# Fourier layers of a vision tower on one core: the inverse row product of a pair in one piece on PE

## The chip, the cores and the metric

One NeuronCore of a Trainium2 chip (trn2). The metric is the device time of one launch in microseconds. The core has engines that run side by side and meet at semaphores: PE (TensorE, matmuls into PSUM), DVE (VectorE), ACT (ScalarE), POOL (GpSimd), and SP, which here issues DMAs. PSUM has 8 banks; the kernel sees them as banks 0 to 7.

## The reference, cut to what matters

Input x has 64 images of 64 x 64 points with 3 channels. The first and longest part, where the change lies, is a lift to 32 channels and four Fourier layers:

```python
def _spectral_conv(x, w):
    B, Cin, H, W = x.shape
    x_ft = jnp.fft.rfft2(x, norm='ortho')
    out = jnp.einsum('bixy,ioxy->boxy', x_ft[:, :, :M1, :M2], w.astype(x_ft.dtype))
    out_ft = jnp.zeros((B, w.shape[1], H, W // 2 + 1), dtype=x_ft.dtype)
    out_ft = out_ft.at[:, :, :M1, :M2].set(out)
    return jnp.fft.irfft2(out_ft, s=(H, W), norm='ortho')
...
x = coords @ fc0_w + fc0_b
x = jnp.transpose(x, (0, 3, 1, 2))
for sw, cw, cb in ((sw0, cw0, cb0), (sw1, cw1, cb1), (sw2, cw2, cb2), (sw3, cw3, cb3)):
    x1 = _spectral_conv(x, sw)
    x2 = jnp.einsum('bchw,oc->bohw', x, cw) + cb[None, :, None, None]
    x = _gelu(x1 + x2)
```

with M1 = M2 = 20 modes kept. Two dense layers bring 32 channels to 64 and to 1; then come one attention layer over rows and a top-6 mixture of 64 experts, both with layer norms. All in float32. Each of the four layers is therefore: transform the rows and then the columns of each image to 20 x 20 modes, multiply the modes by a 32 x 32 matrix each, transform back, add a pointwise convolution, and apply GELU.

## The kernel before, in words

Transforms are matmuls with constant matrices. A pair is two images; there are 32 pairs, and a layer's loop runs over pairs. DVE's 32 x 32 block transposes turn the data between two matmul stages. The stages of one pair, with their names and lines:

- `mix` (PE, L449), once for a whole layer: modes times weights for all images. DVE (L663) and ACT (L704) move the sums to SBUF.
- `turn_modes` (DVE, L632): a pair's modes to `turned_k`.
- `inverse_h` (PE, L462): inverse column product, into banks 4 to 7.
- `turn_inverse` (DVE, L642, two transposes): banks 4 to 7 to `inv_out`, increments `inv_turned`.
- `conv` (PE, L482): the pointwise convolution, into banks 0 to 3, with 16 matmuls. It opens the sums in these banks.
- `inverse_w` (PE, L490): the inverse row product, added onto the same banks. It has four parts p = 0 to 3, one per bank, with 4 matmuls each; each part's last matmul increments `summed`. The trace shows two records for each of these float32 matmuls, so two parts are 16 records.
- GELU (ACT, L711), one per part: bank p to `act_c`, increments `act_set`. Then ACT issues the DMA that stores the pair to DRAM; SP loads it again for the convolution of the next layer, through a ring of four buffers.
- `turn_act` (DVE, L607, two transposes): the new activations to `turned_w`, increments `act_turned`. This and the next four stages are the forward transform for the next layer.
- `dft_w` (PE, L400): row transform, into banks 4 to 7, increments `w_done`.
- `turn_w` (DVE, L618, two transposes): banks 4 to 7 to `turned_h`, increments `w_turned` twice.
- `dft_h` (PE, L412): column transform, into banks 0 and 1, increments `h_done`.
- `turn_h` (DVE, L624): banks 0 and 1 to `modes`, increments `modes_set`.

The order on each engine is written out by hand. For turn j of the loop PE has: `inverse_h` of pair j+1, `conv` and `inverse_w` of pair j, `dft_w` of pair j-2, `dft_h` of pair j-3, with parts 2 and 3 of `inverse_w` behind `dft_w`. DVE has: `turn_inverse` of pair j+1, `turn_modes` of pair j+2, `turn_act` of pair j-1, `turn_w` of pair j-2, `turn_h` of pair j-3. Because banks are shared, PE waits in front of `inverse_h` (L531) for both transposes of `turn_w` of the row transform issued in the turn before, and in front of `conv` (L537) for `turn_h` of the column transform issued in the turn before. It waits in front of `dft_w` (L543, L545) for `turn_act` of its pair and for `turn_inverse` of pair j+1, and in front of `dft_h` (L554) for the GELUs of parts 0 and 1.

Layers 0, 1 and 2 have this full loop, over 35 turns: the row transform is in turns 2 to 33, the column transform in turns 3 to 34. Layer 3 is the last, has no forward transform for a next layer, and its loop has only `inverse_h`, `conv` and `inverse_w`. There the four parts of `inverse_w` lie side by side already, and so they do in turns 0 and 1 of the other layers.

Of the kernel before, what the change touches and what calls it, by code (L numbers as in the profile page):

```python
# [19 lines left out]
PAIRS = IMAGES // 2  # L20
# [168 lines left out]
def tower(nc, banks, h_dram, x, x_turned, fc0, fc0_t, sw, cwt, cb, fc1_w, fc1_b, fc2_w, fc2_b,  # L189
# [4 lines left out]
    with ExitStack() as ctx:  # L194
# [95 lines left out]
        def forward(f, t):  # L290
            return QUARTERS + (f - 1) * PAIRS + t

        def after_turn(f, t):
            return (f - 1) * PAIRS + t + 1

        def after_w_turned(n, ph):
            return 2 * n + ph + 1
# [7 lines left out]
        def after_inv_turned(l, t, i):  # L305
            return l * (2 * PAIRS) + 2 * t + i + 1

        def after_out(l, t, p):
            return (l * PAIRS + t) * 4 + p + 1
# [83 lines left out]
        def _(pe):  # L393

            def dft_w(n):

                for wh in range(2):
                    for i in range(2):
                        for p in range(4):
                            mm = nc.tensor.matmul(banks[i * 64:(i + 1) * 64, 4 + p, :],  # L400
                                                  fwd_w[p * 32:(p + 1) * 32, wh, :],
                                                  turned_w[p * 32:(p + 1) * 32, n % 2, wh, i, :],
                                                  start=(wh == 0), stop=(wh == 1))
                mm.then_inc(w_done, 1)

            def dft_h(n, parity):

                pe.wait_ge(w_turned, after_w_turned(n, 1))
                for ph in range(2):
                    for i in range(2):  # L410
                        for kwh in range(2):
                            mm = nc.tensor.matmul(banks[kwh * 64:(kwh + 1) * 64, i, 0:320],  # L412
                                                  fwd_h[i * 64:(i + 1) * 64, parity, ph, :],
                                                  turned_h[i * 64:(i + 1) * 64, n % 2, ph,
                                                           kwh * 320:(kwh + 1) * 320].rearrange(
                                                      "p (b c m) -> p b m c", c=CH, m=2),
                                                  start=(ph == 0), stop=(ph == 1))
                mm.then_inc(h_done, 1)
# [14 lines left out]
            def mix(l):  # L433

                if l == 0:
                    pe.wait_ge(lift_out, PAIRS)
                else:
                    pe.wait_ge(modes_set, forward(l, PAIRS - 1) + 1)
                for k in range(MIXES):
                    n = l * MIXES + k  # L440
                    pe.wait_ge(mode_w_in[n % RING_W], 16 * (n // RING_W + 1))
                    if k >= 2:
                        pe.wait_ge(mix_out["act"], after_mix(l, k - 2))
                        pe.wait_ge(mix_out["dve"], after_mix(l, k - 2))
                    for m in range(MODES // 2):
                        at = m // 5 * 2 * 512 + m % 5 * 128
                        for kwh in range(2):
                            rows_b = slice(kwh * 64, (kwh + 1) * 64)
                            mm = nc.tensor.matmul(mix_sums(rows_b, k)[:, at:at + 128],  # L449
                                                  mode_w[rows_b, n % RING_W, m, :],  # L450
                                                  modes[rows_b, :, k, 2 * m:2 * m + 2], start=True, stop=True)
                        if m % 5 == 4:
                            mm.then_inc(mixed[m // 5], 1)

            def inverse_h(l, t):

                pe.wait_ge(modes_turned, after_inverse(l, t))
                for i in range(2):
                    for kwh in range(2):
                        for khh in range(2):  # L460
                            b, half = 2 * kwh + khh, khh ^ i
                            mm = nc.tensor.matmul(banks[half * 64:(half + 1) * 64, 4 + 2 * i + kwh, 0:320],  # L462
                                                  inv_h[b * 32:(b + 1) * 32, l % 2, :],
                                                  turned_k[b * 32:(b + 1) * 32, t % 2, i * 320:(i + 1) * 320],
                                                  start=True, stop=True)
                mm.then_inc(inv_h_done, 1)

            def conv(l, t):

                if t > 0:  # L470
                    pe.wait_ge(inv_turned, after_inv_turned(l, t, 1))
                    pe.wait_ge(act_set, after_out(l, t - 1, 3))
                if l == 0:
                    pe.wait_ge(xin_in[t // LIFT_E % 2], 16 * (t // (2 * LIFT_E) + 1))
                else:
                    pe.wait_ge(act_in[t % RING], after_load(l, t))
                for q in range(4):
                    for p in range(4):
                        rows_p = slice(p * 32, (p + 1) * 32)
                        w = first_w[rows_p, t % LIFT_E, :] if l == 0 else conv_w[rows_p, l, :]  # L480
                        src = xin[rows_p, t // LIFT_E % 2, :, q, :] if l == 0 else act_c[rows_p, t % RING, :, q, :]
                        nc.tensor.matmul(banks[q * 32:(q + 1) * 32, p, :], w, src, start=True, stop=False,  # L482
                                         skip_group_check=True)

            def inverse_w(l, t, p):

                for i in range(2):
                    for r in range(2):
                        at = i * 256 + r * 128
                        mm = nc.tensor.matmul(  # L490
                            banks[:, p, at:at + 128],
                            inv_out[:, t % 2, i, p, :, :, r].rearrange("p b o -> p (b o)"),
                            inv_w[:, i, :], start=False, stop=True, skip_group_check=True)
                mm.then_inc(summed, 1)
# [26 lines left out]
            for l in range(LAYERS):  # L521
                mix(l)
                last = l == LAYERS - 1
                inverse_h(l, 0)
                for j in range(PAIRS + (0 if last else 3)):
                    if j == 0:
                        conv(l, 0)
                    if j + 1 < PAIRS:

                        if j >= 3 and not last:  # L530
                            pe.wait_ge(w_turned, after_w_turned(forward(l + 1, j - 3), 1))  # L531
                        else:
                            pe.wait_ge(inv_turned, after_inv_turned(l, j, 1))
                        inverse_h(l, j + 1)
                    if j < PAIRS:
                        if j >= 4 and not last:
                            pe.wait_ge(modes_set, forward(l + 1, j - 4) + 1)  # L537
                        if j > 0:
                            conv(l, j)
                        for p in range(2):  # L540
                            inverse_w(l, j, p)
                    if 0 <= j - 2 < PAIRS and not last:
                        pe.wait_ge(act_turned, after_turn(l + 1, j - 2))  # L543
                        if j + 1 < PAIRS:
                            pe.wait_ge(inv_turned, after_inv_turned(l, j + 1, 1))  # L545
                        elif j >= PAIRS:
                            pe.wait_ge(w_turned, after_w_turned(forward(l + 1, j - 3), 1))
                        dft_w(forward(l + 1, j - 2))
                    if j < PAIRS:
                        for p in range(2, 4):  # L550
                            inverse_w(l, j, p)
                    if 0 <= j - 3 < PAIRS and not last:
                        if j < PAIRS:
                            pe.wait_ge(act_set, after_out(l, j, 1))  # L554
                        else:
                            pe.wait_ge(modes_set, forward(l + 1, j - 4) + 1)
                        dft_h(forward(l + 1, j - 3), (l + 1) % 2)
# [738 lines left out]
```

## Time and profile before

| what | value |
|---|---|
| median of 3 runs | 1860.76 us (1857.05 to 1867.97) |
| the profiled execution, its own time | 1862.68 us |
| its span, first to last instruction | 1860.8 us |
| PE, DVE, ACT busy | 1620.8, 1289.6, 564.5 us |
| mean granted TensorE clock | 0.952 of full speed |
| loops over pairs of layers 0, 1, 2, 3 | 77 to 393, 418 to 729, 755 to 1069, 1094 to 1287 us |

The times of the last line are read off the timeline. In the timeline each row is a run of instructions of one line of the kernel on one engine: start, duration, engine, line, operation, output and inputs with their shapes, the number of records, and in brackets the idle time of the engine before it with what ended it. PE is the matmul stream and PEld the loads of its weights, which overlap it. The end of a matmul is modelled, so a row's duration reaches a little into the next row's; distances between starts are what adds up.

### The profile page before, as it was taken

How to read it: one execution, taken by the hardware profiler on the slowest of the kernel's cores; microseconds unless marked ns; L12 is line 12 of the kernel's file. 1: busy time of each engine (PE TensorE's matmuls, PEld its weight loads, DVE VectorE, ACT ScalarE, POOL GpSimd, SP SyncE). 2: the span in 40 equal slices, each digit the busy share in tenths (PEclk: the TensorE clock that was granted, in tenths of full speed). 3: DMA queues.
4: the chain of work that ended last, by engine and by line, in shares of the span. 5: the costliest groups of instructions: out<-in, count | busy, mean ns of one | idle time of the engine just before them, and what ended most of it. 6: DMA issues, size and time to landing. Idle time of an engine off the chain costs nothing. (4 is left out here: it accounts for less than half of the span.)

```text
span 1860.8 us, 43928 instructions
## 1 busy us (share of the span) xinstructions
PE 1620.8 (87%) x19696; PEld 950.0 (51%) x19696; DVE 1289.6 (69%) x1463; ACT 564.5 (30%) x750; POOL 6.7 (0%) x5
## 2 busy tenths in 40 slices
PE   7999999989999998999999899998666637299994
PEld 2755555566555556655555477775111137243332
DVE  2499888848888885788899645553222264878887
ACT  2332222213222221322222134445666610200000
POOL 1000000000000000000000000000000000000000
PEclk9999999989999999999999999999999965699996
DMA  5323322255655554555555539999555210100000
GB/s 184 94 115 137 137 115 115 114 181 208 228 227 221 220 218 166 191 229 220 219 219 220 200 110 346 360 345 349 189 184 180 80 28 2 70 1 0 0 0 23
DMA packets 62273, 299.94 MB, mean 161 GB/s; under 512 B 21968, under 2 KB 22928, under 8 KB 28048
## 3 DMA queue, kind: packets, MB, share of 16 engines
q1 hardware_dynamic: 43664, 163.01, 25.8%
q10 hardware_dynamic: 18432, 134.23, 17.4%
q8 instruction: 152, 2.49, 0.5%
q14 instruction: 25, 0.20, 0.0%
HBM read 160.90 MB, written 136.31 MB: 160 GB/s over the span
## 5 line engine op out<-in xcount | busy, mean ns | idle before, releaser
L490 PEld LDWEIGHTS slots<-inv_w,inv_out 128*128 128x128 f32 x4096 | 500.6, 197 | 179.4 <-issue 179.4
L711 ACT ACTIVATE act_c<-slots,conv_b 128x512 f32<-128x512 f32 x512 | 352.7, 689 | 740.0 <-PE slots L490 740.0
L490 PE MATMUL slots<-inv_w,inv_out 128*128 128x128 f32 x4096 | 542.2, 287 | 0.0
L642 DVE STREAM_TRANSPOSE inv_out<-slots 128x1024 f32<-128x1024 f32 x256 | 303.9, 1226 | 99.9 <-PE slots L462 99.9
L618 DVE STREAM_TRANSPOSE turned_h<-slots 128x1024 f32<-128x1024 f32 x200 | 237.7, 1227 | 38.1 <-PE slots L400 37.5
L607 DVE STREAM_TRANSPOSE turned_w<-act_c 128x1024 f32<-128x1024 f32 x192 | 225.1, 1210 | 0.0
L400 PE MATMUL slots<-turned_w,fwd_w 32*64 32x512 f32 x3200 | 203.5, 617 | 18.2 <-DVE turned_h L618 10.8
L1178 DVE TENSOR_TENSOR ex_weighted<-slots,ex_y_t 128x512 f32<-128x512 f32 x256 | 157.8, 682 | 33.1 <-PE slots L1048 33.1
L689 DVE TENSOR_SCALAR turned_h<-slots,b 128x512 f32<-128x512 f32 x64 | 48.0, 750 | 158.2 <-PE slots L579 158.2
L722 ACT ACTIVATE inv_out<-slots,b 128x1024 f32<-128x1024 f32 x128 | 135.5, 1111 | 59.4 <-PE slots L570 59.4
L412 PE MATMUL slots<-turned_h,fwd_h 64*64 64x320 f32 x1600 | 138.6, 461 | 5.9 <-DVE modes L624 5.9
L624 DVE STREAM_TRANSPOSE modes<-slots 128x640 f32<-128x640 f32 x96 | 81.3, 847 | 89.2 <-PE slots L412 89.2
L482 PE MATMUL slots<-act_c,conv_w 32*32 32x512 f32 x3072 | 110.9, 599 | 19.6 <-DVE modes L624 15.4
L1060 PE MATMUL slots<-ex_weighted,ex_lattice_w 128*64 128x512 f32 x512 | 123.1, 604 | 0.0
L570 PE MATMUL slots<-act_c,w 32*64 32x512 f32 x1024 | 71.3, 611 | 58.9 <-DVE turned_h L689 58.0
L462 PE MATMUL slots<-turned_k,inv_h 32*64 32x320 f32 x2048 | 102.2, 455 | 13.8 <-DVE turned_k L632 7.2
L400 PEld LDWEIGHTS slots<-turned_w,fwd_w 32*64 32x64 f32 x3200 | 60.9, 134 | 86.8 <-issue 68.6
L632 DVE STREAM_TRANSPOSE turned_k<-modes 128x640 f32<-128x640 f32 x128 | 102.9, 806 | 0.1
L449 PE MATMUL slots<-modes,mode_w 64*64 64x128 f32 x1600 | 94.3, 277 | 3.7 <-DVE modes L624 2.9
L449 PEld LDWEIGHTS slots<-modes,mode_w 64*64 64x64 f32 x1600 | 93.4, 137 | 7.5 <-DVE modes L624 6.0
L663 DVE COPY modes<-slots 128x640 f32<-128x640 f32 x40 | 33.0, 824 | 71.3 <-PE slots L449 71.3
L412 PEld LDWEIGHTS slots<-turned_h,fwd_h 64*64 64x64 f32 x1600 | 51.6, 133 | 55.3 <-issue 11.6
(116 smaller groups left out, 739.8 us busy)
## 6 DMA issues: line engine op xcount, KB each, us to landing
act_scratch<-act_c ACTq DMA_DIRECT2D x128, 1024.0 KB, 4.7
act_c<-act_scratch SPq DMA_DIRECT2D x128, 1024.0 KB, 5.0
mode_w<-in_sw_dram SPq DMA_DIRECT2D x40, 320.0 KB, 2.9
turned_w<-in_x_turned_dram SPq DMA_DIRECT2D x4, 1024.0 KB, 5.8
xin<-in_x_dram SPq DMA_DIRECT2D x4, 1024.0 KB, 7.6
h_scratch<-turned_h SPq DMA_DIRECT2D x256, 4.0 KB
ex_select_raw<-in_k_select_dram SPq DMA_DIRECT2D x1, 2048.0 KB, 9.1
at_h<-h_scratch SPq DMA_DIRECT2D x4, 256.0 KB, 4.6
```

What stands on the lines that cost most here:

```text
L400: mm = nc.tensor.matmul(banks[i * 64:(i + 1) * 64, 4 + p, :], fwd_w[p * 32:(p + 1) * 32, wh, :], turned_w[p * 32:(p + 1) * 32, n % 2, wh, ...
L412: mm = nc.tensor.matmul(banks[kwh * 64:(kwh + 1) * 64, i, 0:320], fwd_h[i * 64:(i + 1) * 64, parity, ph, :], turned_h[i * 64:(i + 1) * 64, ...
L449: mm = nc.tensor.matmul(mix_sums(rows_b, k)[:, at:at + 128], mode_w[rows_b, n % RING_W, m, :], modes[rows_b, :, k, 2 * m:2 * m + 2], start ...
L482: nc.tensor.matmul(banks[q * 32:(q + 1) * 32, p, :], w, src, start=True, stop=False, skip_group_check=True)
L490: mm = nc.tensor.matmul(banks[:, p, at:at + 128], inv_out[:, t % 2, i, p, :, :, r].rearrange("p b o -> p (b o)"), inv_w[:, i, :], start=Fa ...
L607: last = nc.vector.transpose(dst, src)
L618: nc.vector.transpose(dst, src).then_inc(w_turned, 1)
L642: nc.vector.transpose(dst, src).then_inc(inv_turned, 1)
L711: nc.scalar.activation(act_c[:, t % RING, :, p, :], banks[:, p, :].rearrange("p (i m) -> p i m", i=2), ACT.Gelu, bias=conv_b[:, l:l + 1]). ...
L722: nc.scalar.activation(unit[:, n % 2, 2 * half:2 * half + 2, :], banks[:, at:at + 2, :], ACT.Gelu, bias=b1[:, 0:1]).then_inc(unit_set, 1)
L1060: mm = nc.tensor.matmul(slots[j * D:(j + 1) * D, SLOTS - 1, 0:512], lattice_w[:, n, :], weighted[:, n % WB, j * 512:(j + 1) * 512], start= ...
L1178: nc.vector.tensor_tensor(weighted[:, n % WB, cols], slots[:, n % PB, cols], y_t[:, bass.ds(g * SLOT + half * 512, 512)], ALU.mult).then_i ...
```

## The change

PE issues all four parts of a pair's `inverse_w` right after its `conv`, in the turns that have a row transform as in those that have none. `dft_w` and `dft_h` follow, next to each other. The waits stay in front of the stages that they belong to. Nothing changes on the other engines, in the matmuls, the buffers or the DMAs.

```diff
@@ -537,7 +537,7 @@
                             pe.wait_ge(modes_set, forward(l + 1, j - 4) + 1)
                         if j > 0:
                             conv(l, j)
-                        for p in range(2):
+                        for p in range(4):
                             inverse_w(l, j, p)
                     if 0 <= j - 2 < PAIRS and not last:
                         pe.wait_ge(act_turned, after_turn(l + 1, j - 2))
@@ -546,9 +546,6 @@
                         elif j >= PAIRS:
                             pe.wait_ge(w_turned, after_w_turned(forward(l + 1, j - 3), 1))
                         dft_w(forward(l + 1, j - 2))
-                    if j < PAIRS:
-                        for p in range(2, 4):
-                            inverse_w(l, j, p)
                     if 0 <= j - 3 < PAIRS and not last:
                         if j < PAIRS:
                             pe.wait_ge(act_set, after_out(l, j, 1))
```

## Rows read from the trace of the kernel before

**Rows 1.** The page, busy time of PE and DVE, share of the span, instructions

```profile
PE 1620.8 (87%) x19696; PEld 950.0 (51%) x19696; DVE 1289.6 (69%) x1463; ACT 564.5 (30%) x750; POOL 6.7 (0%) x5
```

**Rows 2.** Busy time by stretch: stretch, length, each engine's busy us, granted clock, DMA

```profile
76.00:87.00 11.00, 8.46 (x91) 5.55 (x91) 7.79 (x8) 2.22 (x4) 0.00 (x0) 0.69 0.12 33
...
445.00:707.00 262.00, 254.65 (x3522) 151.55 (x3520) 234.65 (x221) 76.51 (x111) 0.00 (x0) 1.00 0.60 228
...
1300.00:1400.00 100.00, 69.19 (x792) 13.47 (x792) 24.76 (x33) 69.89 (x66) 0.00 (x0) 1.00 0.56 195
```

**Rows 3.** Timeline of layer 1, one period: PE, and DVE's L618 and L624

```profile
508.26 1.15 PE L482 MATMUL slots<-act_c,conv_w 32*32 32x512 f32 x32 [0.25 <-DVE modes L624]
...
509.34 2.15 PE L490 MATMUL slots<-inv_w,inv_out 128*128 128x128 f32 x16
...
511.42 1.97 PE L400 MATMUL slots<-turned_w,fwd_w 32*64 32x512 f32 x32
...
513.33 2.15 PE L490 MATMUL slots<-inv_w,inv_out 128*128 128x128 f32 x16
513.50 2.38 DVE L618 STREAM_TRANSPOSE turned_h<-slots 128x1024 f32<-128x1024 f32 x2
...
515.41 1.36 PE L412 MATMUL slots<-turned_h,fwd_h 64*64 64x320 f32 x16
...
516.70 0.80 PE L462 MATMUL slots<-turned_k,inv_h 32*64 32x320 f32 x16
516.84 0.85 DVE L624 STREAM_TRANSPOSE modes<-slots 128x640 f32<-128x640 f32 x1 [0.95 <-PE slots L412]
...
517.74 1.15 PE L482 MATMUL slots<-act_c,conv_w 32*32 32x512 f32 x32 [0.25 <-DVE modes L624]
```

**Rows 4.** Waits of 500 to 700 us: who waited for whom, us, times, longest

```profile
PE slots L482 <- DVE modes L624: 5.2, 21, 0.3
```

**Rows 5.** Timeline of layer 1, the first row transform and what follows it

```profile
436.61 1.97 PE L400 MATMUL slots<-turned_w,fwd_w 32*64 32x512 f32 x32
...
438.74 2.33 DVE L618 STREAM_TRANSPOSE turned_h<-slots 128x1024 f32<-128x1024 f32 x2
...
441.13 0.80 PE L462 MATMUL slots<-turned_k,inv_h 32*64 32x320 f32 x16 [0.47 <-DVE turned_h L618]
...
441.86 1.19 PE L482 MATMUL slots<-act_c,conv_w 32*32 32x512 f32 x32
...
442.98 2.15 PE L490 MATMUL slots<-inv_w,inv_out 128*128 128x128 f32 x16
```

**Rows 6.** Timeline of layer 3, the piece of four parts and the next PE work

```profile
1104.46 4.04 PE L490 MATMUL slots<-inv_w,inv_out 128*128 128x128 f32 x32
...
1108.42 0.79 PE L462 MATMUL slots<-turned_k,inv_h 32*64 32x320 f32 x16
```

**Rows 7.** Timeline of layer 1, its tail, from pair 31's product to the mixing

```profile
708.42 2.15 PE L490 MATMUL slots<-inv_w,inv_out 128*128 128x128 f32 x16
...
710.50 1.97 PE L400 MATMUL slots<-turned_w,fwd_w 32*64 32x512 f32 x32
...
712.58 2.38 DVE L618 STREAM_TRANSPOSE turned_h<-slots 128x1024 f32<-128x1024 f32 x2 [3.04 <-PE slots L400]
...
716.69 2.33 DVE L607 STREAM_TRANSPOSE turned_w<-act_c 128x1024 f32<-128x1024 f32 x2
...
718.94 2.34 DVE L618 STREAM_TRANSPOSE turned_h<-slots 128x1024 f32<-128x1024 f32 x2
721.21 0.81 DVE L624 STREAM_TRANSPOSE modes<-slots 128x640 f32<-128x640 f32 x1
...
721.43 1.98 PE L400 MATMUL slots<-turned_w,fwd_w 32*64 32x512 f32 x32 [2.39 <-DVE turned_h L618]
...
729.38 15.85 PE L449 MATMUL slots<-modes,mode_w 64*64 64x128 f32 x242 [0.96 <-DVE modes L624]
```

## The prediction

> **What bounds the kernel now.** I read the totals first: PE is busy 87% of the span, DVE 69% [rows 1]. Then the busy time by stretch: in layer 1 (445 to 707 us) PE is busy 254.65 of 262 us at a granted clock of 1.00, its upper level of 2.4 GHz, and DVE 234.65 of 262 [rows 2]. So in the loops over pairs both engines are nearly full, and which of them ends a step has to be read from the order of starts.
>
> That is the timeline [rows 3]. One period is the distance from one convolution to the next, 508.26 to 517.74 = 9.48 us. In it PE does, by starts: convolution 1.08, inverse row product parts 0 and 1 2.08, row transform 1.91, parts 2 and 3 2.08, column transform 1.29, inverse column product 1.04; the sum is the period, so PE is the chain. It has one hole: 0.25 us before the convolution, which waits for DVE's transpose at L624. The waits view has the same hole in all 21 periods of 500 to 700 us, 5.2 us together [rows 4]. There are some 30 such periods in each of layers 0 to 2, and all have this length: the first product of pair 3 of layer 1 starts at 442.98 and that of pair 31 at 708.42 [rows 5, 7], which is 265.44 / 28 = 9.48.
>
> The reader should look at what stands between the row transform and its consumer. The row transform starts at 511.42, and DVE can start turning its result (L618, two transposes, 2.38 us) at 513.50, so it ends at 515.88. PE needs that result when it starts the next inverse column product, at 516.70 [rows 3]: that product writes PSUM banks 4 to 7, which the row transform filled, and waits until L618 has read them. The cover is parts 2 and 3 of the inverse row product (2.08 us) and the column transform (1.29 us), and only 0.8 us of it is to spare.
>
> **The change part by part.** No instruction is added or removed. In the turns of the loop with a row transform and a product, 30 in each of three layers, the matmuls of parts 2 and 3 (16 records of L490) go from behind the row transform to before it.
>
> 1. *The four parts in one piece.* The last layer already has this order. There the piece starts at 1104.46 and the next work at 1108.42, 3.96 us [rows 6], against 2.08 + 2.08 = 4.16 us now [rows 3]. PE's own work falls by 0.20 us a period. The Trainium skill, "TensorEngine Tiling (Array Packing)", Tiling Modes, Key Properties, says that changing the tiling mode drains the engine, and the change takes one of six such changes out of a period; the row agrees in sign and prices it at 0.20 us, and by the rule alone the kernel would get faster.
>
> 2. *The cover that goes.* Now only the column transform stands between the row transform and the inverse column product. Call the row transform's start X. Column transform from X + 1.91 to about X + 3.3. DVE starts L618 at X + 2.08 where it is idle (710.50 to 712.58, [rows 7]) and ends at X + 4.46. PE can start the inverse column product 0.06 us later (the gap of [rows 5], next), X + 4.52. This very sequence exists once in each layer's head, where no column transform is there yet: row transform 436.61, L618 438.74 to 441.07, inverse column product 441.13 with PE idle before it, waiting for L618 [rows 5]. So the stall is about 1.2 us (X + 3.3 to X + 4.52) in each period.
>
> 3. *What is late next.* The convolution follows the inverse column product after 0.73 us (441.13 to 441.86, [rows 5]), X + 5.25. It also waits for L624. That is queued on DVE behind L618 and runs straight after it, 2.27 us after L618's start where that takes 2.34 (718.94, 721.21) and for 0.81 us [rows 7]: its end is X + 2.08 + 2.31 + 0.81 = X + 5.20. Both come out together, so L624 costs nothing more; with the 0.85 us that it takes in [rows 3] it would end at X + 5.24, still before X + 5.25. The column transform itself is done at X + 3.3 and no longer matters: PE, which made L624 wait, now waits for L618.
>
> 4. *The rest of the loop.* Convolution to product takes 1.08 us in [rows 3] and 1.12 in [rows 5]; I take 1.11, since the stall ahead of it makes it more like the second: X + 6.36. The piece takes 3.96, so the next row transform is at X + 10.32. **New period: 2.08 + 2.38 + 0.06 + 0.73 + 1.11 + 3.96 = 10.32 us, 0.84 more than 9.48.**
>
> 5. *The other queues.* DVE's work of a period is 234.65 / 262 x 9.48 = 8.5 us [rows 2], so it has 1.8 us free in 10.32 and is not the bound. The row transform also waits for the two transposes of L642, which follow the inverse column product: as long as L618 (2.38) and begun some 0.9 after X + 4.52 they are ready at about X + 7.8, against X + 10.32: nothing. ACT is busy 29% of the time [rows 2], and its last part is ready long before the next convolution, which now comes 5.25 us after the row transform's start: nothing. The column transform waits for ACT's part 1, which is ready before the piece's parts 2 and 3 are even done: nothing. The DMAs are the same, in more time, and SP and POOL are not moved past. The clock I take as unchanged, see the rivals.
>
> 6. *Head and tail of a layer.* Head: the first row transform starts 3.96 - 2.08 = 1.88 later; DVE is idle then and answers in 2.08 instead of 2.13 [rows 5], so pair 3's product is 1.83 late. Then 28 periods of 0.84 bring pair 31's product to 1.83 + 23.5 = 25.3. Tail, with T that product's start: now 20.96 us to the mode mixing (708.42 to 729.38, [rows 7]), 7.95 of it from the last row transform (721.43). After: row transform T + 3.96, turned at T + 8.42, next row transform T + 8.5; DVE must first do L624 and L607 (2.33) and is free at about T + 11.5, L618 to T + 13.8, last row transform T + 13.9, mixing T + 21.85: 0.9 more. Per layer 25.3 + 0.9 = 26.2; **three layers 79 us.** The last layer has neither transform and is unchanged, and so is all behind it.
>
> The profiled execution took 1862.68 us with a span of 1860.8, so the same execution would come to 1942; from the median of the runs, 1860.76, it is **1940 us** (+4.3%).
>
> Bounds: per period 0.79 (DVE answering 0.05 earlier) to 0.92 (the later L624, the 1.12, and 0.04 more before PE restarts): 3 x 30 x 0.05 = 4.5 us down, 7 up. The tails run partly at the lower clock level already and can shift by some 2 us each, 6 either way.
>
> **The rivals.**
>
> *B, not slower: the merged piece pays and the wait stays covered.* If the next inverse column product did not have to wait for the turn of the row transform just before it (an index one pair older would suffice), the loop would be PE's own work: 9.48 - 0.20 = 9.28, 90 x 0.20 = 18 us less, 1843; with the 0.25 us hole gone too, 90 x 0.45 = 40 less, 1820. It decides where L618 ends before the column transform does: the column transform ends at X + 3.3 and L618 starts at X + 2.08, so the pair would have to take under 1.2 us and takes 2.38. This is what the skill's tiling page would lead to by its drain rule. For it speaks the 0.20 of [rows 6]; against it the head [rows 5], where PE idles until exactly that L618. Chance 0.04 (0.03 faster, 0.01 within the noise).
>
> *C, much slower: the new idle lowers PE's clock.* In 76 to 87 us, after stalls at the head of layer 0, the mean granted clock is 0.69, partly the level of 1.2 GHz; 8.46 us of busy PE hold 8.46 x 0.31 = 2.6 us lost [rows 2]. Once in every period that is 90 x 2.6 = 234, 2174; in one of ten, 1963. Against it: from 1300 to 1400 us PE is busy only 69 of 100 us, idle about 1 us at a time, and the clock is 1.00 [rows 2]; the new loop is busy nearly 90%. Chance 0.04.
>
> *A, the forecast:* 0.92. That the change does not do what it says is not a case of its own: the order on PE is its order in the code.
>
> **How the numbers follow.** The likeliest case gives 1940. Its own range is 1930 to 1953 from the bounds above; the runs of before spread by 11 us, which widens it to 1928 to 1955. That holds over 8 in 10 of the chance, so it does not reach to B or C. About 0.5%, 9 us, is what a measurement can tell: A and C lie far above it, B gives the rest: faster 0.03, same 0.01, slower 0.96.
>
> **What would show it.** In the steady part of layers 0 to 2: a period of 10.3 us; PE's inverse column product (L462) idle about 1.2 us before each start, put down to DVE L618, where it had none; the hole before the convolution gone or under 0.05; L490 in pieces of 32 records over some 4 us; L624's wait for L412 gone, since it runs straight behind L618; DVE idle before L618 for about 1.5 us, waiting for L400; last layer and later stages as before. It would be wrong if the period came out under 9.5 us, if PE's idle stood before L482 or L400, or if the granted clock in 445 to 707 us fell below 1.00.

## The result and the profile after

The changed kernel takes 1939.65 us (median of 4 runs, 1933.91 to 1942.62) against 1860.85 us (median of 4) for the kernel before: a ratio of 1.0415, with a 95% interval of 1.0376 to 1.0455. The forecast was 1940. The profiled execution's span is 1937.1 us.

The page of the kernel after has the same instructions in more time, so a smaller busy share (it answers to [rows 1]):

```profile
PE 1603.4 (83%) x19696; PEld 941.6 (49%) x19696; DVE 1286.9 (66%) x1463; ACT 564.0 (29%) x750; POOL 6.7 (0%) x5
```

Busy time by stretch, for 445 to 707 us as in [rows 2]; PE was busy 254.65 of these 262 us and is now busy 230.37. The mean granted clock is 0.99; one dip at the head of the layer makes up the missing hundredth (last section), and from 472 us on the loop runs at 1.00.

```profile
445.00:707.00 262.00, 230.37 (x3223) 140.68 (x3223) 213.15 (x201) 71.67 (x104) 0.00 (x0) 0.99 0.63 204
```

The waits of 500 to 700 us, as in [rows 4] (who waited for whom, us in total, times, longest):

```profile
PEld slots L462 <- DVE turned_h L615: 35.0, 19, 1.8
DVE turned_h L615 <- PE slots L400: 30.7, 19, 1.6
PE slots L462 <- DVE turned_h L615: 23.9, 19, 1.3
```

Before, PE had no wait in front of the inverse column product here and one of 0.25 us in front of each convolution. Now each of the 19 periods has 1.26 us in front of the inverse column product, for the turn of the row transform (L615 is L618 of the kernel before, three lines up; likewise L621 was L624), and the 0.25 us of PE in front of the convolution are off the list. The other side shows too: DVE now waits 1.6 us for the row transform. PE and DVE wait for each other in turn.

One period in the timeline of layer 1, which answers to [rows 3]:

```profile
472.22 1.97 PE L400 MATMUL slots<-turned_w,fwd_w 32*64 32x512 f32 x32
...
478.59 4.04 PE L490 MATMUL slots<-inv_w,inv_out 128*128 128x128 f32 x32
...
482.55 1.97 PE L400 MATMUL slots<-turned_w,fwd_w 32*64 32x512 f32 x32
...
484.45 1.36 PE L412 MATMUL slots<-turned_h,fwd_h 64*64 64x320 f32 x16
484.63 2.38 DVE L615 STREAM_TRANSPOSE turned_h<-slots 128x1024 f32<-128x1024 f32 x2 [1.62 <-PE slots L400]
486.94 0.81 DVE L621 STREAM_TRANSPOSE modes<-slots 128x640 f32<-128x640 f32 x1
487.07 0.80 PE L462 MATMUL slots<-turned_k,inv_h 32*64 32x320 f32 x16 [1.26 <-DVE turned_h L615]
487.80 1.19 PE L482 MATMUL slots<-act_c,conv_w 32*32 32x512 f32 x32
...
488.92 4.04 PE L490 MATMUL slots<-inv_w,inv_out 128*128 128x128 f32 x32
```

The period is 482.55 - 472.22 = 10.33 us, in all three layers. From the row transform's start X = 482.55 the reader can walk the forecast chain: turn at X + 2.08, product at X + 4.52, convolution at X + 5.25, row product at X + 6.37.

By layers, from the first matmul of one mixing to that of the next: 339.3, 336.4, 339.5 us before and 362.4, 362.5, 363.9 after for layers 0 to 2, and 218.8 and 220.7 for layer 3 with its mixing, to the first matmul of the dense layers. The sum of the differences is 75.5 us of the 76.3 by which the spans differ. This time from the first mixing to the dense layers (called the stage time below: 1234.0 us before, 1309.5 after) is a steadier measure than the total of one run: what lies behind it has the same code in all runs here and took from 573.0 us (the run split_1_3) to 585.7 (longer_turn_before).

### The profile page after: what moved, and what is told of

It is laid out like the page before. It is cut to its first block and busy times, and to the rows that moved or that the text cites. A ratio compares the mean times of both kernels' runs of the same rounds, so it can differ in the third digit from the quotient of the medians.

```text
span 1937.1 us, 43928 instructions
## 1 busy us (share of the span) xinstructions
PE 1603.4 (83%) x19696; PEld 941.6 (49%) x19696; DVE 1286.9 (66%) x1463; ACT 564.0 (29%) x750; POOL 6.7 (0%) x5
## 5 line engine op out<-in xcount | busy, mean ns | idle before, releaser
L490 PEld LDWEIGHTS slots<-inv_w,inv_out 128*128 128x128 f32 x4096 | 493.8, 197 | 108.6 <-issue 108.6
L490 PE MATMUL slots<-inv_w,inv_out 128*128 128x128 f32 x4096 | 518.2, 285 | 0.0
L615 DVE STREAM_TRANSPOSE turned_h<-slots 128x1024 f32<-128x1024 f32 x200 | 238.0, 1228 | 186.7 <-PE slots L400 186.7
L482 PE MATMUL slots<-act_c,conv_w 32*32 32x512 f32 x3072 | 116.2, 616 | 10.1 <-DVE modes L621 4.0
L462 PEld LDWEIGHTS slots<-turned_k,inv_h 32*64 32x64 f32 x2048 | 30.4, 131 | 181.2 <-DVE turned_h L615 159.4
L449 PE MATMUL slots<-modes,mode_w 64*64 64x128 f32 x1600 | 88.7, 267 | 3.7 <-DVE modes L621 2.9
L449 PEld LDWEIGHTS slots<-modes,mode_w 64*64 64x64 f32 x1600 | 87.8, 130 | 6.2 <-DVE modes L621 4.7
L621 DVE STREAM_TRANSPOSE modes<-slots 128x640 f32<-128x640 f32 x96 | 77.7, 809 | 4.4 <-PE slots L412 4.4
```

The lines of the kernel that those rows point to most:

```text
L449: mm = nc.tensor.matmul(mix_sums(rows_b, k)[:, at:at + 128], mode_w[rows_b, n % RING_W, m, :], modes[rows_b, :, k, 2 * m:2 * m + 2], start ...
L490: mm = nc.tensor.matmul(banks[:, p, at:at + 128], inv_out[:, t % 2, i, p, :, :, r].rearrange("p b o -> p (b o)"), inv_w[:, i, :], start=Fa ...
L615: nc.vector.transpose(dst, src).then_inc(w_turned, 1)
```

## The experiments

The theory: the row product's parts 2 and 3 had covered DVE's turn of the row transform, and the loss is PE's wait for it. Rival 1: the new order is slow on PE itself (neighbouring transforms, or one long piece). Rival 2: the row transform comes too late in the period, whatever DVE takes.

### The turn made shorter, in both orders

The edit is in `turn_w`, in the changed kernel and in the one before. The second transpose of a turn for layers 1 to 3 then covers an eighth of its columns, so these kernels leave out the rest of the forward transform's second half; PE's matmuls stay the same.

```diff
                     dst = turned_h[:, n % 2, ph, :].rearrange("p (b c m) -> p c b m", c=CH, m=2)
+                    if n >= QUARTERS and ph == 1:
+                        src, dst = src[:, :, 0:2, :], dst[:, :, 0:2, :]
                     nc.vector.transpose(dst, src).then_inc(w_turned, 1)
```

> The changed order, with the second transpose of the turn after each row transform of layers 1 to 3 cut to an eighth of its columns (the part it leaves out of the forward transform is missing in the output). Theory (the loss is PE's wait for this turn, once its cover is gone): the turn takes about 1.35 us instead of 2.38, the wait before the inverse column product shrinks from 1.26 to about 0.3 us and the period from 10.33 to about 9.3 us; total about 1845. Rival 1 (row and column transform next to each other, or the four parts in one piece, are slow on PE itself): the period stays at 10.3, total 1935 to 1940. Rival 2 (the row transform comes too late in the period whatever DVE takes): also 10.3.

> The control for the shortened turn, in the order before the change, with the same part of the transform left out. Theory: the turn is covered there by parts 2 and 3 and the column transform, so a shorter one brings nothing; the period stays 9.48 with the 0.25 us hole before the convolution, total 1857 to 1863. If the turn were a cost in both orders, this one would fall by about 1 us a period as well, to about 1770.

Measured: 1841.3 us in the changed order and 1853.1 in the old one (one run each; 1861.4 for the kernel before on that chip). Periods: 9.40 and 9.48 us. The timeline of the changed order with the short turn, DVE's turn and PE's next product:

```profile
524.49 1.45 DVE L617 STREAM_TRANSPOSE turned_h<-slots 128x1024 f32<-128x1024 f32 x2 [1.63 <-PE slots L400]
...
525.99 0.80 PE L462 MATMUL slots<-turned_k,inv_h 32*64 32x320 f32 x16 [0.32 <-DVE turned_h L617]
```

The turn is 0.93 us shorter (1.45 for 2.38), the wait 0.94 shorter (0.32 for 1.26), and the period 0.93 shorter. All the loss goes with DVE's work, though PE's order is that of the change: rivals 1 and 2 are out. In the old order the same cut leaves the period at 9.48, with the hole before the convolution; the timeline of that run has

```profile
516.98 1.15 PE L482 MATMUL slots<-act_c,conv_w 32*32 32x512 f32 x32 [0.25 <-DVE modes L626]
...
526.46 1.15 PE L482 MATMUL slots<-act_c,conv_w 32*32 32x512 f32 x32 [0.24 <-DVE modes L626]
```

The total of that run fell some 4 us further than expected, and the stage time by 9 (1224.8). That is a balance of several things. Layers 0 to 2 are 18.3 us shorter together. In layer 1, for instance, the tail from pair 31's inverse column product to the mixing is 2.3 us shorter, since there the turn is on the path in either order [rows 7], and the mixing, up to the first inverse column product, is 1.6 us shorter, because it ran at a granted clock of 1.00 and not 0.93. Layer 3 is 9.2 us longer, and there the convolution waited 9.3 us in all for the loads of `act_c`.

### The turn made longer, in both orders

```diff
+        spare = sb("spare", [128, 512])
...
                     dst = turned_h[:, n % 2, ph, :].rearrange("p (b c m) -> p c b m", c=CH, m=2)
-                    nc.vector.transpose(dst, src).then_inc(w_turned, 1)
+                    if n >= QUARTERS and ph == 0:
+                        nc.vector.transpose(spare[:].rearrange("p (b c m) -> p c b m", c=CH, m=2), src[:, :, 0:8, :])
+                    nc.vector.transpose(dst, src).then_inc(w_turned, 1)
```

> The changed order with one more transpose (512 columns into a spare buffer, about 0.67 us) at the head of each turn after a row transform. Theory: all of it lands on the path, period about 11.0 us, total about 1940 + 90 x 0.67 = 2000. Rivals 1 and 2: DVE has 1.8 us free in each period, so the period stays at 10.33 and the total at 1940.

> The same added transpose in the order before the change. Theory: the 0.8 us to spare between the end of the turn and the inverse column product take it in, period 9.48 to 9.55, total 1858 to 1868. If the cover were less than the trace shows, the period would grow by up to 0.67, total up to 1921.

Measured: 2056.7 and 1881.1 us. In the old order the period is still 9.48: the timeline has the longer turn and PE's product without a wait of its own.

```profile
525.14 0.72 DVE L621 STREAM_TRANSPOSE spare<-slots 128x512 f32<-128x512 f32 x1
525.78 2.34 DVE L622 STREAM_TRANSPOSE turned_h<-slots 128x1024 f32<-128x1024 f32 x2
...
528.34 0.79 PE L464 MATMUL slots<-turned_k,inv_h 32*64 32x320 f32 x16
```

The turn ends at 528.12, 0.2 us ahead of the product: the old order had room for it, as [rows 3] said. The total missed the expected 1868 by 13 us, but the stage time grew by 5.7 only (1239.7); the other 12.6 lie behind the layers, where nothing was changed.

In the changed order most periods are 10.93, the expected kind (0.60 more), but of the 84 distances between inverse column products in the loops of layers 0 to 2, 31 are 12.40 to 12.50, and so the total is 57 us over the expectation. Here is such a long one, from the timeline, and the busy time by stretch around it:

```profile
541.51 0.80 PE L464 MATMUL slots<-turned_k,inv_h 32*64 32x320 f32 x16 [1.85 <-DVE turned_h L619]
542.24 1.64 PE L484 MATMUL slots<-act_c,conv_w 32*32 32x512 f32 x32
543.80 5.12 PE L492 MATMUL slots<-inv_w,inv_out 128*128 128x128 f32 x32
548.86 1.97 PE L402 MATMUL slots<-turned_w,fwd_w 32*64 32x512 f32 x32
```

```profile
470.00:700.00 230.00, 194.10 (x2612) 122.02 (x2608) 175.57 (x176) 57.90 (x84) 0.00 (x0) 0.94 0.53 178
...
542.00:548.00 6.00, 6.00 (x72) 4.48 (x59) 5.55 (x6) 1.38 (x2) 0.00 (x0) 0.72 0.44 183
```

After the wait of 1.85 us the granted clock falls for part of the convolution and the row product, to a mean of 0.72 over 6 us: convolution to row transform takes 6.62 us where it takes 5.08 at full clock. This is rival C of the prediction, which the change itself does not set off in its loop. A smaller addition (256 columns for 512, in the changed order) tries a PE wait between 1.26 and 1.85 us:

> The changed order with a smaller added transpose (256 columns, about 0.3 to 0.4 us) at the head of each turn. Theory of the wait alone: period 10.33 + 0.3 to 0.4, total 1967 to 1976. With the larger one (0.6 us, idle stretches of 1.85 us on PE) the granted clock fell to 0.94 in the loops and the total to 2057 instead of 2000; if stretches of about 1.6 us suffice for that too, some periods show 12 us or more, the clock in the loops is under 1.00, and the total is above 1990.

Measured: 1971.2 us, one run; period 10.66. Of 84 distances two are long, 13.40 and 12.20 us, and both come at the head of a layer, behind a wait of 2.87 and 2.88 us. Its timeline has PE idle 1.59 us a period at a granted clock of 1.00:

```profile
540.38 0.45 DVE L618 STREAM_TRANSPOSE spare<-slots 128x256 f32<-128x256 f32 x1 [1.64 <-PE slots L402]
540.75 2.34 DVE L619 STREAM_TRANSPOSE turned_h<-slots 128x1024 f32<-128x1024 f32 x2
...
543.15 0.80 PE L464 MATMUL slots<-turned_k,inv_h 32*64 32x320 f32 x16 [1.59 <-DVE turned_h L619]
```

So the length of the turn passes one to one into the period: 1.45, 2.38, 2.71 and 2.98 us of DVE work (the last two from the addition's start to the turn's end) give 9.40, 10.33, 10.66 and 10.93 us.

### Where the row transform stands among the parts

The kernel before with k parts ahead of the row transform and 4 - k behind it, k = 3, 1 and 0, called split_3_1, split_1_3 and split_0_4 (its own k is 2, that of the change 4):

```diff
-                        for p in range(2):
+                        for p in range(3):
                             inverse_w(l, j, p)
...
-                        for p in range(2, 4):
+                        for p in range(3, 4):
                             inverse_w(l, j, p)
```

> Three parts before the row transform, one behind it. Theory: the path 2.08 + 2.38 + 0.06 + 0.73 + 1.11 plus three parts (about 3.0) gives 9.4 us, with a wait of about 0.2 before the inverse column product in place of the hole before the convolution; total 1850 to 1862. A linear price per part moved (half of the loss of the change) would give 9.9 us and 1900.

> One part before the row transform, three behind it. Theory: the row transform now waits for the turn of the inverse column product (ready 3.33 us after that product starts, PE gets there after about 3.2): 0.1 to 0.2 us more, the hole before the convolution stays; period 9.55 to 9.7, total 1868 to 1882.

> The row transform first, all four parts in one piece behind it: the piece is as whole as in the change, but on the covering side. Theory: the other turn (of the inverse column product) loses its cover instead: the row transform starts 3.33 us after that product, period 3.33 + 1.91 + 3.97 + 1.29 = about 10.5 us, the wait standing before the row transform; total about 1950. Rival 2 (only a late row transform costs): 9.3 to 9.5 us, 1845 to 1861.

| parts ahead | 0 | 1 | 2 (before) | 3 | 4 (after) |
|---|---|---|---|---|---|
| period, us | 10.59 | 9.65 | 9.48 | 9.48 | 10.33 |
| time, us | 1952.9 | 1870.8 | 1860.9 | 1861.9 | 1939.7 |

(The times for 0 and 1 are of one run each.) For k = 1 period and time lie in the expected ranges. For k = 3 the ratio to the kernel before is 0.9995 (0.9974 to 1.0015), with a period 0.08 over the expected 9.4, since the convolution came 0.85 us after the product and not 0.73: the column transform, later here than in the change, brought L624's end to X + 5.32. The price is not the same for every part moved: the third part costs nothing and the fourth 0.85 us. For k = 0 the loss stands on the other side, as expected; the waits of 500 to 700 us and the timeline of that run:

```profile
PE slots L400 <- DVE inv_out L642: 23.5, 19, 1.2
```

```profile
526.69 1.98 PE L400 MATMUL slots<-turned_w,fwd_w 32*64 32x512 f32 x32 [1.24 <-DVE inv_out L642]
...
528.60 4.04 PE L490 MATMUL slots<-inv_w,inv_out 128*128 128x128 f32 x32
```

Its row product is as much in one piece as in the change, but behind the row transform; what lost its cover is DVE's other turn of banks 4 to 7, that of the inverse column product. The four parts cover two turns, one on each side of the row transform, and the kernel before shares them out evenly.

These runs also price the piece. By starts, at full clock and with no wait behind it, a piece of 1, 2, 3 and 4 parts takes 1.14 (533.41 to 534.55 in split_3_1), 2.08, 3.02 (528.49 to 531.51 there) and 3.96 us: 0.94 for a part and 0.20 for each piece.

### The transforms left as neighbours, the cover given back

Parts 0 and 1, row transform, column transform, then parts 2 and 3 (the run two_w_h_two):

```diff
                         dft_w(forward(l + 1, j - 2))
-                    if j < PAIRS:
-                        for p in range(2, 4):
-                            inverse_w(l, j, p)
                     if 0 <= j - 3 < PAIRS and not last:
...
                         dft_h(forward(l + 1, j - 3), (l + 1) % 2)
+                    if j < PAIRS:
+                        for p in range(2, 4):
+                            inverse_w(l, j, p)
```

> Parts 0 and 1, row transform, column transform, then parts 2 and 3: row and column transform stay next to each other as in the change, but parts 2 and 3 (2.08 us) stand between the row transform and the next inverse column product again, and now also between the column transform and the next convolution. Theory: both turns on DVE are covered, the 1.26 us wait and the old 0.25 us hole are gone, period 9.23 us (PE's own work), total 1861 - 22 = about 1838 (1833 to 1850). Rival 1 (neighbouring transforms are slow in themselves): 10.3 us, 1935 to 1940.

Measured: 1861.3 us, ratio 0.9993 (0.9971 to 1.0015), period 9.49. Rival 1 falls once more, the 1.26 us are gone. But the expected gain of 22 us did not come. Timeline:

```profile
529.64 0.81 DVE L624 STREAM_TRANSPOSE modes<-slots 128x640 f32<-128x640 f32 x1
...
530.53 0.79 PE L462 MATMUL slots<-turned_k,inv_h 32*64 32x320 f32 x16
530.64 0.69 ACT L711 ACTIVATE act_c<-slots,conv_b 128x512 f32<-128x512 f32 x1 [0.25 <-PE slots L490]
531.43 2.38 DVE L642 STREAM_TRANSPOSE inv_out<-slots 128x1024 f32<-128x1024 f32 x2 [0.98 <-PE slots L462]
...
531.58 1.15 PE L482 MATMUL slots<-act_c,conv_w 32*32 32x512 f32 x32 [0.26 <-ACT act_c L711]
```

L624 ended at 530.45, before the product even began, and yet the convolution comes 1.05 us after the product, as it did when L624 ended 0.05 us ahead of it [rows 3]. The trace now names the GELU of part 3, which ended at 531.33, 0.25 us earlier. Two runs followed this up. The first, three_w_h_one, moves only part 3 behind the transforms, so that its GELU ends early:

```diff
-                        for p in range(2):
+                        for p in range(3 if 2 <= j and not last else 4):
                             inverse_w(l, j, p)
...
                         dft_h(forward(l + 1, j - 3), (l + 1) % 2)
+                    if 2 <= j < PAIRS and not last:
+                        inverse_w(l, j, 3)
```

(The loop of parts 2 and 3 between the transforms is gone there as well.)

> Parts 0 to 2, row transform, column transform, part 3, next inverse column product. Theory: that product is bound by the turn of the row transform (X + 4.52 from the row transform's start X), part 3 fills all but 0.26 us of the gap, its GELU ends at about X + 5.1 and no longer holds the convolution, L624 ends at X + 5.2, so the convolution is at X + 5.25; with 1.11 and three parts (3.02) the period is 9.38 us, 0.10 less than before, total about 1852 to 1858. If the 0.25 us ahead of the convolution is not a wait for DVE or ACT but PE's own, it comes back here and the period is 9.5 or more, total about 1863.

Measured: 1861.5 us, ratio 1.0004 (0.9979 to 1.0028), period 9.49. Period and total are those of the second reading, a delay of PE's own, although one part of the first is met: in the timeline the product waits for the turn, to 543.20, which is X + 4.52 as expected, but the convolution follows after 0.89 us (0.86 or 0.87 in other periods), not 0.73.

```profile
541.88 1.21 PE L490 MATMUL slots<-inv_w,inv_out 128*128 128x128 f32 x8
...
543.07 0.81 DVE L623 STREAM_TRANSPOSE modes<-slots 128x640 f32<-128x640 f32 x1
543.12 0.69 ACT L710 ACTIVATE act_c<-slots,conv_b 128x512 f32<-128x512 f32 x1 [3.64 <-PE slots L490]
...
544.09 1.15 PE L482 MATMUL slots<-act_c,conv_w 32*32 32x512 f32 x32
```

The GELU ended at 543.81 and L623 at 543.88; with 0.05 us after L623 the convolution could have started at 543.93. So ACT is not the cause, and no other engine accounts for the last 0.16 us. The second run, modes_wait_early, takes the order of two_w_h_two and moves one wait instruction of PE, for L624, from between product and convolution to ahead of the product:

```diff
                             pe.wait_ge(w_turned, after_w_turned(forward(l + 1, j - 3), 1))
+                            if j >= 4:
+                                pe.wait_ge(modes_set, forward(l + 1, j - 4) + 1)
...
-                        if j >= 4 and not last:
+                        if j == PAIRS - 1 and not last:
                             pe.wait_ge(modes_set, forward(l + 1, j - 4) + 1)
```

> The order parts 0 and 1, row transform, column transform, parts 2 and 3, with PE's wait for L624 moved from between the inverse column product and the convolution to ahead of that product. In the run two_w_h_two L624 ended 0.08 us before the product started, so nothing has to wait longer. There the convolution still came 1.05 us after the product's start, though L624 had long ended and the GELU had ended 0.25 us before; in layer 3, with one wait instruction fewer at that place, it comes after 0.90. If the additional wait instruction there is what costs, the period is 9.34 us and the total 0.15 x 90 = 13 us less, about 1847. If it is something else (the GELU's signal, or PE's own change of tiles), the period stays 9.49 and the total about 1861.

Measured: 1851.1 us against 1862.6 for the kernel before on the same chip, ratio 0.9936 (0.9914 to 0.9959); period 9.36, stage time 1217.8 us. This version is faster than both kernels, by a small margin. Timeline:

```profile
543.76 2.15 PE L490 MATMUL slots<-inv_w,inv_out 128*128 128x128 f32 x16
...
545.95 0.69 ACT L713 ACTIVATE act_c<-slots,conv_b 128x512 f32<-128x512 f32 x1 [0.26 <-PE slots L490]
...
546.00 0.80 PE L462 MATMUL slots<-turned_k,inv_h 32*64 32x320 f32 x16
...
546.74 1.18 PE L482 MATMUL slots<-act_c,conv_w 32*32 32x512 f32 x32
```

The product now starts 2.24 us after parts 2 and 3 instead of 2.08, and the convolution 0.74 after the product instead of 1.05: 0.15 less together. The convolution starts 0.10 us after the GELU's end, so it does not need 0.25 for that. The place of a wait whose semaphore had long been set is worth 0.13 to 0.15 us a period.

One reading puts these orders together. Take the moment at which PE could have begun the inverse column product if nothing had held it, and measure from there to the convolution. That is 1.04 us in the kernel before [rows 3], 1.05 in two_w_h_two, 1.04 in split_3_1 (534.55 + 1.29 for the column transform, to 536.88) and 1.07 in three_w_h_one (541.88 + 1.14, to 544.09), whether L624 ended early or late. It is 0.90 in layer 3 and 0.90 in modes_wait_early (543.76 + 2.08, to 546.74), though there L626 may have held the product for a part of it. In the code PE passes four wait instructions between product and convolution in the first group (for L624, L642, the GELU and the load) and three in the second. So about 1.05 us looks like a least distance of PE's own, with some 0.15 of it for the one wait, and it would explain why four orders come out at 9.48 or 9.49 us: the rest of the period is PE's work in each, two pieces of the row product among it. How PE handles a wait so that it costs is not shown, and no run changed the number of the others.

### The wait by halves

The changed order, with PE waiting for each half of the turn only before it writes that half's banks (wait_by_half):

```diff
-            def inverse_h(l, t):
+            def inverse_h(l, t, turned=None):
...
                 for i in range(2):
+                    if turned is not None:
+                        pe.wait_ge(w_turned, after_w_turned(turned, i))
                     for kwh in range(2):
...
                         if j >= 3 and not last:
-                            pe.wait_ge(w_turned, after_w_turned(forward(l + 1, j - 3), 1))
+                            inverse_h(l, j + 1, forward(l + 1, j - 3))
```

> The changed order, but the inverse column product waits for each half of the turn of the row transform just before it writes that half's banks, instead of for both at its start. Theory: the product now starts at X + 3.3 and its second half at X + 4.52, so it ends 0.3 to 0.4 us earlier; but L624, queued behind L618 on DVE, still ends at X + 5.2 and becomes what the convolution waits for: period 10.30 to 10.35, total 1935 to 1943. If the turn alone sets the loop and L624 does not matter, the period falls to about 10.0 and the total to 1908.

Measured: 1931.7 us, period 10.30. Timeline:

```profile
545.07 0.77 PE L464 MATMUL slots<-turned_k,inv_h 32*64 32x320 f32 x8 [0.22 <-DVE turned_h L617]
545.98 0.81 DVE L623 STREAM_TRANSPOSE modes<-slots 128x640 f32<-128x640 f32 x1
546.11 0.77 PE L464 MATMUL slots<-turned_k,inv_h 32*64 32x320 f32 x8 [0.27 <-DVE turned_h L617]
546.84 1.15 PE L484 MATMUL slots<-act_c,conv_w 32*32 32x512 f32 x32
```

Half of the product is done during the turn, and next to nothing is gained. L623 ends at 546.79 and the convolution starts 0.05 us behind it, as expected if L623 binds. But this run does not prove that: each half of the product takes 0.77 us by its row, where the whole takes 0.80, and so the second half alone also puts the convolution 0.73 us behind the turn. The two come out together, as step 3 said, and which of them holds the convolution stays open. The total is 3 us under the expected range, within what one run leaves open.

## Why the prediction was right

1. *The piece.* 3.96 us forecast; 478.59 to 482.55 in the timeline of after is 3.96. The 0.20 us it saves are in the new period. The Trainium skill's rule of the drain ("TensorEngine Tiling (Array Packing)", Tiling Modes, Key Properties) gave the right sign for this term, and the 0.20 us that every piece costs agree with it, though no run here shows that a drain is what they are; the total went the other way, because PE was no longer what bound the loop.
2. *The cover.* Product at X + 4.52 forecast, 4.52 measured; wait 1.2 forecast, 1.26 measured. That this wait is the loss is shown by the turn made shorter and longer: the period follows it one to one.
3. *What is late next.* L621 ended at X + 5.20 and the convolution started at X + 5.25, both as forecast. wait_by_half leaves open which of the two, the product or L621, held the convolution.
4. *The rest.* Convolution to product 1.12 (1.11 forecast), period 10.33 (10.32).
5. *Other queues.* DVE idles 1.62 us before the turn (about 1.5 forecast). In 500 to 700 us there is no other new wait, and none among the longest is put down to a DMA, though the median from issue to landing of the stores rose from 4.7 to 8.5 us. In layer 3, which was to stay as it was, the convolution waited twice for a load of `act_c`, 2.1 us together, where it had no such wait before.
6. *Head and tail.* From the first inverse column product of layer 1 to pair 3's convolution it is 1.88 us more (441.86 - 418.58 before, 465.56 - 440.40 after), 1.83 forecast. From pair 31's product to the mixing it is 21.39 us, 21.85 forecast:

```profile
757.55 4.04 PE L490 MATMUL slots<-inv_w,inv_out 128*128 128x128 f32 x32
...
778.94 1.32 PE L449 MATMUL slots<-modes,mode_w 64*64 64x128 f32 x20 [0.97 <-DVE modes L621]
```

The sum was 79 us for three layers; the three differ by 23.1, 26.1 and 24.5 us, 73.7 together, and layer 3 by 1.9 where I had 0. Most of the difference lies in where the lower clock level falls in the two traces. The mixings of layers 1 and 2 took 25.6 and 26.3 us before, at granted clocks of 0.93 and 0.91, and 24.0 each after (from their first matmul to the first inverse column product). From the last row transform to the next mixing it is 3.3 us less in the three layers together. Against that, two dips at the heads of layers 1 and 2 cost 1.6 and 1.5 us. Layer 3's mixing is 1.6 us shorter in the same way, and its loop 3.5 us longer, 2.1 of it the waits for loads.

So the mechanism and the period came out as forecast, but that the total came out at 1939.65 where the forecast was 1940 is partly luck: the layers of the profiled executions fall 3.5 us short of the sum, and the medians differ by 78.8 us where these two executions differ by 76.3. All this is within the bounds given.

Rival B failed where it was said to: the turn is longer than the cover that is left. Rival C did not happen in the loop at 1.26 us of idle, and did at 1.85. "The clock I take as unchanged" was right for the loop only. One of the signs of being wrong, a granted clock under 1.00 in 445 to 707 us, was met by the letter (0.99), through the dip at the head of the layer, which the prediction did not foresee. One more thing was taken too simply, though the forecast did not rest on it: rival B's floor of 9.48 - 0.45 counted the 0.25 us hole before the convolution as a pure wait for L624. With L624 early, the hole stayed.

## What to carry to other kernels

Between two engines that hand a buffer back and forth, count for each handover what stands between producer and consumer on the engine that waits, and compare it with the other engine's time; here work could be moved out of a cover without cost only as far as the cover had time to spare, and beyond that each microsecond of turn cost a microsecond of period. Merging the pieces of a block for a saving on its own engine (0.20 us here) was a bad trade, because the block covered a turn on both sides. Look in the trace for a head, a tail or a last layer where the new order already stands: here they gave all the terms of the sum to 0.01 to 0.1 us.

## What the runs showed of the hardware that I had not expected

A wait instruction of PE between the inverse column product and the convolution cost 0.13 to 0.15 us a period, although its semaphore had been set 1.1 us before the convolution started: moved to ahead of the product, it took the period from 9.49 to 9.36 us and the kernel from no gain to 0.6% less (0.9936). What it costs at its new place does not show: the product started 0.16 us later there, but also 0.09 us after the end of L626 (L624 of the kernel before), so it may have waited for that.

The granted clock in a loop with a repeated PE idle stretch was 1.00 at 1.26 us in 10.33 (after) and at 1.59 in 10.66, and 0.94 at 1.85 in 10.93, where over a third of the periods (31 of 84) fell partly to the lower level of 1.2 GHz and took 12.5 us. One longer stretch came before a dip in the changed kernel too, at the head of layer 1, where PE had been idle 2.54 us; timeline, and busy time by stretch:

```profile
464.83 0.80 PE L462 MATMUL slots<-turned_k,inv_h 32*64 32x320 f32 x16 [2.54 <-DVE turned_h L615]
465.56 1.96 PE L482 MATMUL slots<-act_c,conv_w 32*32 32x512 f32 x32
467.45 4.83 PE L490 MATMUL slots<-inv_w,inv_out 128*128 128x128 f32 x32
```

```profile
465.00:472.00 7.00, 7.00 (x79) 4.90 (x74) 5.36 (x5) 1.99 (x3) 0.00 (x0) 0.76 0.39 144
```

Convolution to row transform took 6.66 us there against 5.08 in the loop. That is one dip of 1.6 us in the layer; at the head of layer 1 in the kernel before, where the idle time was 0.47 us [rows 5], there was none. The idle stretch alone does not decide it, though. At the head of layer 2 PE was idle 2.55 us and the clock fell as well (the next distance between products is 11.78 us, not 10.33), but at the head of layer 0 it was idle 2.54 us, from the row transform at 97.95 to the product at 102.47, and the granted clock from 98 to 112 us is 1.00, with the next product at 112.80 after the usual 10.33. With the smaller addition all three heads had PE idle for 2.87 or 2.88 us; two of them were followed by a dip and one was not. What else decides it, these runs do not show.
